# First stage of a Hyena block: another order of loads and blocks, x1 evicted by two engines, its bias added later

## The chip, the cores and the metric

The kernel runs on one core of a Trainium2 chip. The metric is the device time of one execution in microseconds. The engines of the core are TensorE (PE), VectorE (DVE), ScalarE (ACT), GpSimd (POOL) and SyncE (SP); each works through its own instructions in program order and waits on semaphores for the others.

## The reference, cut to what matters

```python
xn = _layernorm(x)                          # x: 4096 tokens x 256 channels
# attention branch: a second layernorm (gamma, beta), then
proj = (layernorm(xn) @ W_in + b_in)        # 256 -> 3 x 256: v, x1, x2
y = v
for kern, xi in ((k0, x1), (k1, x2)):       # 128 taps, causal, one filter per channel
    y = fft_conv(y, kern) * xi
out_attn = xn + (y @ W_out + b_out)
# feed-forward branch: weights are int32 / 127
h = silu(xn @ wg.T) * (xn @ wu.T)           # 256 -> 768
out = x + out_attn + h @ wd.T               # 768 -> 256
```

## The kernel before

Tokens are cut into 32 blocks of 128. The **first stage** goes over the blocks one by one and does four kinds of work.

1. **Blocks.** DVE takes mean and variance of x (`layernorm_stats`, in batches of 4, 8, 8, 8 and 4 blocks, `CUTS`). POOL makes the scales of a batch (`layernorm_scales`, lines 979 to 991; `r_ready` is given at line 987, `r2_ready` at line 991). ACT normalises a block (line 563), PE transposes it (line 290), ACT rounds it to float16 (line 567), DVE takes the remainder (`split_x`, line 703), and ACT writes a copy with reversed token order (`reverse_x`, line 574). PE then projects the block: x1 in `project_x1` (six products of 256 columns), and the first 32 channels of v and x2 in `project` (six products of 64 columns). A block is transposed four steps ahead of its projection (`p = b - 4`).
2. **x1.** DVE evicts x1 block by block (line 713, 256 values per partition): it multiplies by the block's scale, adds the bias row and writes to `x1y2`, where neighbouring channels are 32 values apart. `bias` is itself made by POOL (line 1039).
3. **v and x2.** After every eight blocks DVE scales one bank (line 721), POOL adds a bias (`add_bias`, line 999), ACT rounds (line 579), POOL takes the remainder (`split_v`, line 1005).
4. **Weights and constants.** Column norms of the input weights (PE), their scales (DVE, `column_scales`) and the split in two float16 parts; the filter taps, which POOL scales and splits (`taps`) and SP writes to memory and reads back as bands; the maxima of the FFN weights (DVE, line 816), a chain of tiny DVE operations (`ffn_constants`, lines 759 to 775), and nine pairs of FFN weight tiles. POOL scales a pair (line 1012), PE transposes it (line 323), ACT rounds it (line 583), DVE takes the remainder (line 726). One buffer and one bank hold a pair, so the pairs go one after another.

Whether the FFN weights need a third product is decided on the chip: PE loads a flag that `ffn_constants` makes and takes one of two copies of the code that follows. This branch stands after step 17 of the first stage (`FORK`), so both copies hold the rest of that stage.

The **main loop** goes over 16 groups of 16 channels (G). Each group has two convolutions (bands times v, then bands times y1), three FFN steps of 512 tokens x 128 hidden units, and the projections of later channels. POOL multiplies by x1 (`gate_1`, line 1062, two halves) and by x2 (`gate_2`, line 1068), adds biases for the later channels, and works on the residual (`residual`, lines 1031 and 1032, two blocks a group). The **last stage** projects y to the output and stores it.

All order is written out by hand. SP issues the loads: x in five parts, the taps, the FFN weights, then the two output tensors; ACT issues W_in, gamma, beta and b_in. PE order in step b is: transpose block b, project block b - 4, transpose a pair.

## Time and profile before

| | us |
|---|---|
| median of 3 runs (lowest, highest) | 374.84 (373.56, 377.35) |
| the profiled execution | 376.25 |
| its span, first to last instruction | 374.4 |

| engine | busy us (share of the span) | instructions |
|---|---|---|
| PE | 314.0 (84%) | 4940 |
| DVE | 253.6 (68%) | 522 |
| ACT | 183.2 (49%) | 383 |
| POOL | 196.6 (53%) | 268 |

The shares are means over the three stages. The first stage projects its first block at 28.75 us and its last one until 92.8 us; the first convolution starts at 98.44 us. The last group of the main loop ends near 345 us. So the first stage with its way into the main loop takes about a quarter of the span.

### The profile page before, as it was taken

The numbers are of one execution on the slowest core, as the hardware profiler recorded it, in microseconds if no ns is written. First come the engines' busy times: TensorE is split into PE (matmuls) and PEld (weight loads), VectorE is DVE, ScalarE is ACT, GpSimd is POOL, SyncE is SP. The second block draws the span as 40 slices with busy tenths as digits, with TensorE's granted clock in tenths as the row PEclk, the third lists the DMA queues.
The fourth block names the chain that finished last, engine by engine and source line by source line (L and its number), as shares of the span: only waits on it lengthen the run. The fifth ranks groups of instructions, "written<-read, shape, count | busy, mean of one in ns | idle before, by whom it ended". The sixth has DMA issues, their size and how long they took to land.

```text
span 374.4 us, 11762 instructions
## 1 busy us (share of the span) xinstructions
PE 314.0 (84%) x4940; PEld 244.9 (65%) x4940; DVE 253.6 (68%) x522; ACT 183.2 (49%) x383; POOL 196.6 (53%) x268
## 2 busy tenths in 40 slices
PE   0637593988699889999999999999997997857995
PEld 0426462877477667677777777777765775645994
DVE  1894994788356766666667657667658666576986
ACT  1465363896253434433534444434443344427993
POOL 3697085466566746747657667567564573210000
PEclk9977867899899999999999999999999899996999
DMA  8996100033268758687786786886886768500345
GB/s 251 340 306 218 65 1 4 2 92 137 56 242 374 249 218 320 256 321 279 268 355 237 283 355 227 306 333 222 315 315 247 268 202 339 199 0 3 115 168 170
DMA packets 22072, 81.00 MB, mean 216 GB/s; under 512 B 2050, under 2 KB 13186, under 8 KB 13826
## 3 DMA queue, kind: packets, MB, share of 16 engines
q1 hardware_dynamic: 21026, 79.04, 57.7%
q10 hardware_dynamic: 992, 1.18, 1.0%
q8 instruction: 41, 0.67, 0.7%
q14 instruction: 13, 0.11, 0.1%
HBM read 75.50 MB, written 4.72 MB: 214 GB/s over the span
## 4 chain that ended last, share of the span: by engine, by line
DVE 28%; ACT 18%; POOL 17%; PE 17%; issue 15%; DMA 3%; POOLq 0%; DVEq 0%; SPq 0%; ACTq 0%
PE bank_c L270 6%; DVE sgh L830 6%; ACT hhl L613 5%; DVE vx L721 4%; POOL vx L999 3%; PE bank_g L270 3%; PE bank_u L270 3%; ACT vx L663 3%; POOL x1y L1068 3%; DMA res<-in_L_attn_x 3%; DVE ybuf L851 3%; POOL ybuf L1062 3%; DVE hhl L835 2%; DVE res L842 2%; POOL vhl L1005 2%
## 5 line engine op out<-in xcount | busy, mean ns | idle before, releaser
L270 PE MATMUL bank_d<-wd,hhl 128*128 128x256 f16 x384 | 87.3, 271 | 4.5 <-DVE hhl L835 4.1
L270 PEld LDWEIGHTS bank_p<-wq,xT 128*128 128x128 f16 x1536 | 72.4, 99 | 18.2 <-issue 2.2
L270 PE MATMUL bank_p<-wq,xT 128*128 128x64 f16 x1536 | 82.2, 195 | 1.8 <-issue 1.8
L270 PEld LDWEIGHTS bank_c<-vhl,bands 128*128 128x128 f16 x1024 | 52.7, 98 | 28.5 <-issue 13.4
L270 PE MATMUL bank_c<-vhl,bands 128*128 128x64 f16 (+3 forms) x1024 | 61.4, 187 | 10.2 <-POOL vhl L1005 7.9
L270 PE MATMUL bank_u<-xT,wgu 128*128 128x512 f16 x192 | 66.7, 381 | 0.0
L270 PE MATMUL bank_g<-xT,wgu 128*128 128x512 f16 x192 | 66.7, 381 | 0.0
L270 PEld LDWEIGHTS bank_c<-ybuf,bands 128*128 128x128 f16 x1024 | 51.7, 96 | 19.2 <-issue 3.2
L270 PE MATMUL bank_c<-ybuf,bands 128*128 128x64 f16 (+3 forms) x1024 | 60.1, 184 | 2.7 <-DVE ybuf L855 2.7
L835 DVE TENSOR_TENSOR hhl<-sgh,hhl 128x512 f16<-128x512 f32 x48 | 39.0, 812 | 34.1 <-ACT hhl L613 34.1
L613 ACT CAST hhl<-sgh 128x512 f16<-128x512 f32 x48 | 29.6, 617 | 54.9 <-DVE sgh L830 54.6
L999 POOL TENSOR_TENSOR vx<-vx,bias 128x512 f32<-128x512 f32 x32 | 34.4, 1074 | 41.7 <-DVE vx L721 40.9
L607 ACT ACTIVATE sgh<-bank_g,cst 128x512 f32<-128x512 f32 x48 | 32.7, 681 | 25.7 <-PE bank_g L270 25.6
L270 PEld LDWEIGHTS bank_d<-wd,hhl 128*128 128x128 f16 x384 | 37.0, 97 | 5.9 <-ACT hhl L613 4.4
L270 PE MATMUL bank_c<-wq,xr 128*128 128x256 f16 x192 | 31.3, 308 | 8.3 <-DVE x1y L713 4.5
L1068 POOL TENSOR_TENSOR x1y<-ybuf,vx 128x256 f32<-128x256 f32 x32 | 27.3, 867 | 19.6 <-DVE ybuf L851 19.6
L830 DVE SCALAR_TENSOR_TENSOR sgh<-bank_u,cst,sgh 128x512 f32<-128x512 f32 x48 | 35.6, 742 | 0.0
L851 DVE TENSOR_TENSOR ybuf<-bank_c,xr 128x256 f32<-128x256 f32 x64 | 26.6, 416 | 13.0 <-ACT xr L621 12.5
L1062 POOL TENSOR_TENSOR ybuf<-ybuf,x1y 128x256 f32<-128x256 f32 x32 | 23.3, 728 | 21.2 <-DVE ybuf L851 21.2
L1005 POOL TENSOR_TENSOR vhl<-vx,vhl 128x256 f16<-128x256 f32 x32 | 24.3, 758 | 15.1 <-ACT vhl L579 15.1
L621 ACT COPY xr<-bank_c 128x256 f32<-128x256 f32 x64 | 23.6, 369 | 16.9 <-PE bank_c L270 16.9
L270 PEld LDWEIGHTS bank_c<-wq,xr 128*128 128x128 f16 x192 | 20.5, 111 | 13.6 <-issue 5.3
(167 smaller groups left out, 541.6 us busy)
## 6 DMA issues: line engine op xcount, KB each, us to landing
bands<-taps_seq SPq DMA_DIRECT2D x64, 1024.0 KB, 7.6
out<-res SPq DMA_DIRECT2D x8, 512.0 KB, 2.9
res<-in_L_attn_x SPq DMA_DIRECT2D x3, 1024.0 KB, 10.4
res<-in_L_attn_x SPq DMA_DIRECT2D x2, 512.0 KB, 8.3
bands<-in_L_attn_W_in ACTq DMA_DIRECT2D x1, 768.0 KB, 5.7
bands<-in_L_ffn_w_gate SPq DMA_DIRECT2D x1, 768.0 KB, 10.0
bands<-in_L_ffn_w_up SPq DMA_DIRECT2D x1, 768.0 KB, 10.2
vx<-in_L_ffn_w_down SPq DMA_DIRECT2D x1, 768.0 KB, 10.5
```

What stands on the lines that cost most here:

```text
L270: return nc.tensor.matmul(o, w, m, start=start, stop=stop, skip_group_check=True)
L607: nc.scalar.activation(sgh[:, n % 2, :], bank_g[:, :], ACT.Silu, scale=c(C_GS)).then_inc(sg_ready, 1)
L613: nc.scalar.copy(hhl[:, n % 3, 0, :], sgh[:, n % 2, :]).then_inc(hh_ready, 1)
L621: nc.scalar.copy(conv_lo[:, h, :, :], o[:, 1, :, :]).then_inc(lo_copied, 1)
L721: nc.vector.tensor_tensor(vx[:, r % 2, :, :, blocks].rearrange("p i c b -> p (i c) b"), bank_p[n % 2][:, :].rearrange("p (b c) -> p c b", ...
L830: nc.vector.scalar_tensor_tensor(out=sgh[:, n % 2, :], in0=bank_u[:, :], scalar=c(C_HS), in1=sgh[:, n % 2, :], op0=ALU.mult, op1=ALU.mult) ...
L835: nc.vector.tensor_tensor(hhl[:, n % 3, 1, :], sgh[:, n % 2, :], hhl[:, n % 3, 0, :], ALU.subtract).then_inc(hl_ready, 1)
L851: nc.vector.tensor_tensor(y1f[:, h * CH:(h + 1) * CH, :], o[:, 0, :, :], conv_lo[:, h, :, :], ALU.add).then_inc(c_added, 1)
L999: nc.gpsimd.tensor_tensor(tile, tile, off, ALU.add).then_inc(vx_ready, 1)
L1005: nc.gpsimd.tensor_tensor(vhl[:, r % 2, 1, :, blocks], vx[:, r % 2, 0, :, blocks], vhl[:, r % 2, 0, :, blocks], ALU.subtract).then_inc(vl_ ...
L1062: nc.gpsimd.tensor_tensor(y1f[:, chans, :], y1f[:, chans, :], x1y2[:, G * CG + h * CH:G * CG + (h + 1) * CH, :], ALU.mult).then_inc(y1_rea ...
L1068: nc.gpsimd.tensor_tensor(x1y2[:, G * CG + h * CH:G * CG + (h + 1) * CH, :], y1f[:, h * CH:(h + 1) * CH, :], vx[:, r % 2, 1, g * CG + h * ...
```

## The change

It edits the first stage and one place of the main loop.

- **Loads.** SP issues W_in right behind the first part of x; the parts of x become 4, 4, 8, 8 and 8 blocks, with the taps, w_gate, w_up and w_down between them. ACT issues gamma, beta and b_in only.
- **Order of blocks.** A block is projected eight steps after its transposition (`LAG`) in place of four. The beta product stands before the first block on PE. DVE's statistics are cut into pieces, mostly one block a step. Column scales, taps, the three maxima and the FFN constants stand at other steps, the pairs start at step 20 (`PAIR0`).
- **Second half of the input weights.** POOL multiplies rows 128 to 255 by gamma and by the column scale (two operations) and takes their low part; DVE did both before.
- **Normalising.** Blocks 20 to 31 are normalised by POOL, blocks 0 to 19 by ACT.
- **x1.** Pairs 0 to 5 of blocks are evicted by ACT (a copy with a scale, two of 256 values a pair), pairs 6 to 15 by DVE (one operation of 512 values a pair). No bias is added there.
- **Bias of x1.** POOL adds it in `add_x1_bias`, 512 values for each of the 16 groups: for group 0 behind the first stage, for group G + 1 behind `gate_2` of group G. `gate_1` waits for it.
- **Residual.** The residual of blocks 0 to 3 stands behind the last `split_v` of the first stage.
- **Branch.** PE's branch stands at the stage's end, behind the wait for all pairs.

```diff
-    CUTS = (0, 4, 12, 20, 28, NB)
+    CUTS = (0, 4, 8, 16, 24, NB)
+    LAG = 8
+    NA = 20
+    JA = 6
+    PAIR0 = 20
...
+            load_x(0)
+            sp.dma_start(win[:, :, :], W_in.rearrange("(k p) n -> p k n", p=P)).then_inc(win_loaded, 16)
+            load_x(1)
+            load_x(2)
...
-                p = b - 4
-                if p >= 0:
+                p = b - LAG
+                if 0 <= p < NB:
                     project_x1(p)
...
             def body(general):
-                for b in range(FORK, NB + 4):
-                    first_stage(b)
-                pe.wait_ge(unit_h, PAIRS)
-                pe.wait_ge(unit_l, PAIRS)
                 for G in range(NG):
...
-            FORK = 17
-            for b in range(FORK):
+            beta_weights()
+            for b in range(NB + LAG):
                 first_stage(b)
+            pe.wait_ge(unit_h, PAIRS)
+            pe.wait_ge(unit_l, PAIRS)
...
+            def evict_x1(j):
+                act.wait_ge(x1_mm, 2 * j + 2)
...
+                    last = nc.scalar.activation(x1y2[:, :, b:b + 1].rearrange("p c o -> p (c o)"), o, ACT.Copy, scale=col(r2r, b))
+                last.then_inc(x1a_ready, 1)
...
-                nc.vector.scalar_tensor_tensor(out=x1y2[:, :, b:b + 1].rearrange("p c o -> p (c o)"), in0=o, scalar=col(r2r, b),
-                                               in1=bias[:, D:2 * D], op0=ALU.mult, op1=ALU.add).then_inc(x1_ready, 1)
...
+                nc.vector.tensor_tensor(x1y2[:, :, pair], bank_c[j % 2][:, :].rearrange("p (b c) -> p c b", b=2), scales,
+                                        ALU.mult).then_inc(x1v_ready, 1)
...
-            for b in range(1, NB + 7):
-                if b in (3, 10, 13):
-                    layernorm_stats({3: 2, 10: 3, 13: 4}[b])
+            for b in range(1, NB + LAG + 5):
+                if b == 1:
+                    layernorm_stats(4, 8)
+                elif b in (2, 3, 4):
+                    layernorm_stats(3 * b + 2, min(3 * b + 5, 16))
+                elif b + 11 < NB:
+                    layernorm_stats(b + 11, b + 12)
...
+            def normalise(b):
...
+                pool.wait_ge(x_tp, b - 3)
+                nc.gpsimd.tensor_scalar(xn[:, b % 4, :], res[:, b, :], col(r1, b), col(nmr, b), ALU.mult, ALU.add).then_inc(xnp_ready, 1)
...
+            def add_x1_bias(G):
...
+                nc.gpsimd.tensor_tensor(tile, tile, off, ALU.add).then_inc(x1_biased, 1)
...
+                if b == 21:
+                    layernorm_scales(4)
+                if NA <= b + 2 < NB:
+                    normalise(b + 2)
...
+            add_x1_bias(0)
...
+                pool.wait_ge(x1_biased, G + 1)
...
+                if G < NG - 1:
+                    add_x1_bias(G + 1)
```

Two places in the instruction order carry most of the prediction. POOL from the first pair on (line 1012 before, line 1057 now; the names `lns` are layernorm scales, `vx` is the pair's buffer or a bank of v and x2, `ybuf` the normalised block). Before:

```order
L1012 TENSOR_SCALAR vx<-bands,cst 128x512 x2
L1005 TENSOR_TENSOR vhl<-vx,vhl 128x32x8
L1012 TENSOR_SCALAR vx<-bands,cst 128x512
L999 TENSOR_TENSOR vx<-vx,bias 128x64x8
L1012 TENSOR_SCALAR vx<-bands,cst 128x512 x3
```

Now:

```order
L1057 TENSOR_SCALAR vx<-bands,cst 128x512
L1022 TENSOR_SCALAR lns<-mv 128x8
L1023 TENSOR_TENSOR lns<-lns,minus_half 128x8
L1024 TENSOR_TENSOR lns<-mv,lns 128x8
L1025 TENSOR_SCALAR lns<-lns 128x8
L1026 TENSOR_TENSOR lns<-mv,lns 128x8
L1027 TENSOR_TENSOR lns<-lns 128x8
L1028 TENSOR_SCALAR lns<-lns 128x8
L1029 TENSOR_TENSOR lns<-lns,minus_half 128x8
L1030 TENSOR_SCALAR lns<-lns 128x8
L1036 TENSOR_SCALAR ybuf<-res,lns 128x256 x2
L1057 TENSOR_SCALAR vx<-bands,cst 128x512
```

Behind the first pair POOL now has a whole batch of scales and then two normalised blocks, where it went from pair to pair before.

PE around the branch (`COMPARE_AND_BRANCH`; `bank_c` takes x1 or a convolution, `bank_p` v and x2, `bank_g` and `bank_u` the FFN). Before:

```order
L323 MATMUL bank_d<-ident,vx 128x128 x4
L503 TENSOR_LOAD flag
L503 ISA x2
L504 COMPARE_AND_BRANCH
L290 MATMUL bank_d<-ident,ybuf 128x128 x2
L270 MATMUL bank_c<-wq,xr 128x256 x6
L270 MATMUL bank_p<-wq,xT 128x64 x6
```

Now:

```order
L282 MATMUL bank_c<-wq,xr 128x256 x6
L282 MATMUL bank_p<-wq,xT 128x64 x6
L523 TENSOR_LOAD flag
L523 ISA x2
L524 COMPARE_AND_BRANCH
L282 MATMUL bank_g<-xT,wgu 128x512 x6
L282 MATMUL bank_u<-xT,wgu 128x512 x6
```

The branch moved from the middle of the blocks to between the last projection and the first FFN step.

## Rows read from the trace of the kernel before

**Rows 1.** busy time by engine in three stretches: length, each engine's busy us (instructions), PEclk, DMA share, GB/s.

```profile
28.75:59.50 30.75, 21.34 (x186) 16.86 (x187) 25.16 (x81) 16.62 (x37) 17.38 (x30) 0.75 0.24 86
63.50:92.80 29.30, 26.71 (x294) 23.77 (x295) 22.55 (x46) 24.65 (x55) 16.93 (x15) 0.93 0.21 74
98.40:344.60 246.20, 228.47 (x4180) 173.83 (x4181) 160.14 (x268) 105.23 (x215) 136.70 (x176) 0.97 0.69 258
```

**Rows 2.** timeline of DVE: start, us, line, operation, out<-in, count, [idle before].

```profile
9.45 0.16 DVE L779 SCALAR_TENSOR_TENSOR gnorm<-gb 128x4 f32<-128x4 f32 x1 [0.81 <-DMA gb<-in_L_attn_beta]
...
15.88 1.02 DVE L735 SCALAR_TENSOR_TENSOR bands<-bank_c,bands 128x384 f32<-128x384 f32 x2
...
53.08 0.17 DVE L759 COPY cst<-bank_d 128x3 f32<-128x3 f32 x1
...
56.88 0.15 DVE L775 TENSOR_SCALAR flag<-cst 128x1 int32<-128x1 f32 x1
```

**Rows 3.** timeline of PE, the same columns.

```profile
14.84 3.58 PE L270 MATMUL bank_p<-bands,vx 128*128 128x384 f32 x8
...
28.75 1.44 PE L270 MATMUL bank_c<-wq,xr 128*128 128x256 f16 x6 [3.83 <-issue]
...
30.78 1.49 PE L270 MATMUL bank_c<-wq,xr 128*128 128x256 f16 x6
...
63.52 0.66 PE L290 MATMUL bank_d<-ident,ybuf 128*128 128x128 f32 x2 [3.49 <-issue]
...
84.28 0.82 PE L270 MATMUL bank_c<-wq,xr 128*128 128x256 f16 x6
...
85.36 0.82 PE L270 MATMUL bank_c<-wq,xr 128*128 128x256 f16 x6
...
92.81 1.03 PE L270 MATMUL bank_g<-xT,wgu 128*128 128x512 f16 x4
...
98.44 2.71 PE L270 MATMUL bank_c<-vhl,bands 128*128 128x64 f16 x64 [3.74 <-POOL vhl L1005]
```

**Rows 4.** timeline of ACT, one block's normalise, round and reverse.

```profile
82.60 0.61 ACT L563 ACTIVATE ybuf<-res,lns 128x256 f32<-128x256 f32 x1
83.10 0.37 ACT L567 CAST xT<-bank_u 128x256 f16<-128x256 f32 x1
...
83.87 0.61 ACT L563 ACTIVATE ybuf<-res,lns 128x256 f32<-128x256 f32 x1
```

**Rows 5.** groups of POOL instructions before 98.4 us: busy us, mean ns, idle before.

```profile
L1012 POOL TENSOR_SCALAR vx<-bands,cst 128x512 f32<-128x512 int32 x6 | 9.4, 1570 | 11.1 <-PE bank_d L323 11.1
...
L999 POOL TENSOR_TENSOR vx<-vx,bias 128x512 f32<-128x512 f32 x4 | 4.3, 1078 | 1.8 <-DVE vx L721 1.8
...
L1031 POOL TENSOR_SCALAR res<-res,lns 128x256 f32<-128x256 f32 x4 | 2.2, 558 | 0.0
...
L1039 POOL TENSOR_TENSOR bias<-vhl 128x768 f32<-128x768 f32 x1 | 1.8, 1814 | 0.0
```

**Rows 6.** durations of line 655 on ACT: ns min/median/max.

```profile
L655 ACT ACTIVATE vx<-x1y,lns x32: 722/796/909, 338.3 to 366.4; 128x256 f32<-128x256 f32 x32
```

**Rows 7.** timeline of POOL, two batches of layernorm scales.

```profile
15.10 0.86 POOL L983 TENSOR_SCALAR lns<-mv 128x8 f32<-128x8 f32 x1 [2.29 <-DVE mv L695]
...
46.78 0.24 POOL L983 TENSOR_SCALAR lns<-mv 128x8 f32<-128x8 f32 x1 [11.13 <-DVE mv L695]
...
49.36 0.24 POOL L987 TENSOR_SCALAR lns<-lns 128x8 f32<-128x8 f32 x1
...
50.49 1.67 POOL L991 TENSOR_TENSOR lns<-lns,minus_half 128x8 f32<-128x8 f32 x1
```

**Rows 8.** timeline of POOL in group 1 of the main loop.

```profile
115.36 0.73 POOL L1062 TENSOR_TENSOR ybuf<-ybuf,x1y 128x256 f32<-128x256 f32 x1
117.05 0.72 POOL L1062 TENSOR_TENSOR ybuf<-ybuf,x1y 128x256 f32<-128x256 f32 x1 [0.96 <-DVE ybuf L851]
```

**Rows 9.** durations of line 835 on DVE: ns min/median/max.

```profile
L835 DVE TENSOR_TENSOR hhl<-sgh,hhl x48: 691/716/1245, 102.1 to 335.3; 128x512 f16<-128x512 f32 x48
```

More of the change, by code:

```diff
@@ L252, in _ @@
                         if G == 0 and v == 0:
-                            sp.wait_ge(wql_ready, 2)
+                            for k in range(KD):
+                                sp.wait_ge(wql_ready[k], 1)
                         elif G == 0:
@@ L562, in normalise @@
                     act.wait_ge(x_tp, b - 3)
[L563 removed]
+                nc.scalar.activation(xn[:, b % 4, :], res[:, b, :], ACT.Identity, bias=col(nmr, b), scale=col(r1, b)).then_inc(xna_ready, 1)
             def round_x(b):
@@ L586, in _ @@
             normalise(1)
-            for b in range(NB + 6):
-                if b + 2 < NB:
+            for b in range(NB + LAG + 5):
+                if b + 2 < NA:
                     normalise(b + 2)
@@ L1059, in gate_1 @@
+            add_x1_bias(0)
+            pool.wait_ge(bout_loaded, 16)
+            for b in range(TPC):
+                residual(b)
             def gate_1(G, h):
```

266 lines of the change are left out of this document (154 added, 112 removed).

## The prediction

> **What bounds the kernel now.** I read the stretches by engine first, then the timelines of PE, ACT, DVE and POOL in the first stage, then POOL's and DVE's rows of the main loop. In the main loop PE is busy 228.5 of 246.2 us [rows 1], so little is to be won or lost there unless a new wait reaches PE. In the first stage PE is busy 21.3 of 30.75 us in the first part and 26.7 of 29.3 us in the second, at a granted clock of 0.75 and 0.93 [rows 1]. The first part is held by DVE, 25.2 of 30.75 us busy, the second by ACT, 24.65 of 29.3 us [rows 1]. ACT's step there is normalise 0.50, then round and reverse 0.77, together 1.27 us a block [rows 4]. PE needs 1.08 us a block at the full clock and 2.03 at the lower level (starts of x1's products at 84.28 and 85.36, at 28.75 and 30.78 [rows 3]). PE also stands still for 3.49 us at the branch, before 63.52 [rows 3]. The end of the stage is the first convolution at 98.44 us, 3.74 us after PE ran dry [rows 3].
>
> **The change, as one path.** I follow the new order along what each step waits for.
>
> 1. *Until the scales of blocks 8 to 15.* DVE starts gamma's norm at 9.45 us, on the arrival of beta [rows 2]. ACT issues these loads one place earlier, which I count as 0.5 us; they may land up to 2.5 us earlier as the large W_in is no longer ahead of them. The column scales start at 15.88 us now [rows 2]. In the new order they stand behind the remainder of block 0, and that stands behind the beta product, 3.58 us [rows 3], which was behind the first transpositions. With the norm products from 11.5 to 12.8 us this gives 12.8 + 3.3 + 1.2 = 17.3 for their start and 19.5 for the scales. Then POOL's second multiplication of 768 values, 1.8 us [rows 5], its small batch (2.2 us to `r_ready`), ACT's block 4 and the two casts, 2.4 us: 25.9. DVE's remaining statistics and the low half, 3.1 us, give 29.0, and POOL's scales of eight blocks take 46.78 to 49.6, 2.8 us [rows 7]: 31.8 at the late end, 29.3 at the early end. I take 30.5, in the middle. This part gives nothing: the first projection follows 1.3 us later, at 31.8, where it is at 28.75 now [rows 3].
> 2. *Steps 6 to 17.* ACT paces: 12 x 1.27 = 15.2 us [rows 4] and four evictions of a pair. The trace shows no ACT copy from a bank to places 32 values apart. Below it is bounded by the 0.26 us that rounding adds to a step, a bank read of the same size (from the 0.77 of rows 4, less a reverse of 0.51), above by 0.80 us for ACT's strided read [rows 6]. I take 0.55, the middle, so 1.1 a pair and 4.4 in all: 50.1. The ends move this by 2 us either way. DVE's pieces fit beside it: its statistics are unchanged in number, its maxima stand in three steps, and from pair 6 on one operation replaces two.
> 3. *The constants.* DVE's chain runs from 53.08 to 57.03 [rows 2], 3.95 us, and comes at step 18, behind 0.5 us of step work: 54.6. Here PE is held for about 2 us, no more, as it is two blocks ahead.
> 4. *Steps 20 to 31.* Now POOL paces. It must do one pair (1.57), a batch of scales (46.78 to 52.16, 5.4 us [rows 7]), nine normalised blocks of 0.56, four more pairs, one bias of 1.08 and one `split_v` of 0.67: 1.57 + 5.4 + 5.0 + 6.3 + 1.1 + 0.7 = 20.0 us [rows 5, 7]. Block 31 is normalised at 74.6, 1.9 us a step up to there, more than ACT's 0.8 and PE's 1.3.
> 5. *Pairs 5 to 8.* POOL and PE take turns on one buffer. Pair 5 ends at 76.2; three more turns of 1.57 for POOL, 0.5 for PE and 0.2 for the signals are 6.8, and the bias between them 1.1: 84.1. PE's transposition, 0.5, and its last two blocks, 2 x 0.83 (1.08 less the transposition's 0.25), end at 86.2. Before it was 92.8.
> 6. *Into the main loop.* The v path needs 0.7 + 1.08 + 0.4 + 0.67 and signals, 3.2 us. It is hidden by PE's own: the branch, 3.49 us [rows 3], then gate and up products, of which four took 1.03 us at the full clock at 92.81 [rows 3], 1.7 to 1.9 for all eight, and 3.4 at the lower level, at which PE came back from this stall. The convolution starts at 86.2 + 6.9 = 93.1, which is 5.3 us earlier. The lower level is then mostly used up: the first 64 products took 2.7 us at 98.44 [rows 3], partly at the lower level, and I estimate 2.0 here, 0.7 less. So 6.0 us are won. The residual of four blocks that held `split_v` now stands behind it: POOL is free at 89.4 + 1.1 + 4 x 1.3 = 95.7, where the first sum is ready at 95.1; the second `gate_1` comes later anyway, so this costs nothing.
> 7. *Main loop.* POOL gets 15 additions of 1.08 us [rows 5]. Today the first `gate_1` of a group follows the residual without idle time and the second has 0.96 us of idle before it [rows 8]. An addition of 1.08 uses up that idle and leaves 0.12 us. Only in the odd groups does the path to PE's next wait go through it: 7 x 0.12 = 0.9 us. The ends are 0 and 15 x 1.08 = 16.2.
>
> Sum: 6.0 - 0.9 = **5.1 us less**. Against the profiled execution, 376.25 us, that is 371.1. The runs shown have their median 1.4 us lower, so I forecast **369.7 us**.
>
> **Two rules beside the rows.** On step 7, DVE's low half of h, line 835, takes 0.69 us at the least and 1.25 us at the most [rows 9], in the same group of instructions, and long ones lie beside POOL's gates. The Trainium skill, page "SBUF — State Buffer", section "SBUF: two separate sides", says that a DVE operation with two SBUF inputs and a GpSimd operation hold one pair of ports for the whole instruction, and that the other is blocked, not slowed. By that rule each added POOL operation could also hold up a DVE one, up to its whole length; it is the second rival below. The trace agrees in kind: 1.25 us is not explained by the operation's size. On step 6 the row shows 3.49 us without work behind the branch. The Trainium skill, page "Runtime: NRT & Kernel Launch", section "Instruction fetch mechanics", says that a taken branch to code outside the window that is held forces a fetch before PE goes on. By it the stall would follow the branch to its new place whatever the code there; the row bears out that there is one.
>
> **The rivals.** (A) The forecast as above: 0.50.
> (B) *The front goes faster*: evictions on ACT at 0.26 us (2 us up to step 17) and gamma and beta early (1.2 us). Everything behind moves, since POOL's work waits for the constants: 369.7 - 3.2 = 366.5. For it speaks that ACT's bank reads are its shortest operations. 0.13.
> (C) *POOL is slower than its own rows.* A small scale operation took 0.86 us at 15.10 beside DVE and 0.24 at 46.78 [rows 7], the same form. Two batches, two multiplications and a subtraction now stand in front of the first projection. Stretched by 2 us there and 2 us in steps 20 to 31, the time is 373.7, no change that can be told. 0.17.
> (D) *The additions reach the path*, with the blocking: 15 x 1.08 = 16.2 in place of 0.9 makes 385.0. The kernel is slower than before from (5.1 + 0.9) / 15 = 0.4 us a group on. Against it speak the idle times of POOL [rows 8]. 0.10.
> (E) *TensorE stays at its lower level.* PE goes idle for up to 4 us at POOL's batch in step 21, and after 3.49 us of idle it came back at the lower level [rows 3]. If it held that over steps 23 to 39, its step would be 2.03 + 0.23 with a transposition and 1.6 + 0.23 without: 62.1 + 9 x 2.3 + 8 x 1.83 = 97.4 as the stage's end in place of 86.2, and 380.9 in all. It decides against the change from half of these steps on. Against it: at the lower level PE would be busy all the time, and in such a stretch from 63.5 us on it returned to the full clock (0.93 over the stretch [rows 1]). 0.10.
>
> **How the numbers follow.** Of a kernel like this a measurement can tell about 1% from no change, 3.7 us, so faster is below 371.1 and slower above 378.6. A's own range is 366 to 373; 0.45 of its 0.50 lie below 371.1. With B that is 0.58. Within 1% are C, the rest of A and 0.05 of the mild forms of D and E: 0.27. The rest, 0.15, is slower. The range takes in B and, for the unsure length of steps 20 to 39, 3 us below it, 363.5, and on the other side C and the mild forms of D and E, up to 378.5; beyond the two ends lie some 0.15 to 0.2.
>
> **What would show it.** In the trace after: the first projection near 32 us, later than now; ACT without gaps up to about 50 us; POOL nearly without idle time from 55 to 76 us, with PE waiting for its normalised blocks; PE's last projection near 86 us, then 3.5 us of nothing, then the FFN step at the lower level and the convolution near 93 us; in the main loop the second `gate_1` right behind the first one and the loop's length as now, 246 us, within 2 us. A first projection beyond 35 us, an eviction on ACT of 0.8 us, or a loop longer by over 4 us would each take most of the gain; the forecast is wrong as well if PE's stall at the branch is not there.

## The result, and the profile after

| | before | after |
|---|---|---|
| median of 4 runs (lowest, highest) | 374.20 (372.04, 377.35) | 379.97 (378.27, 381.08) |
| ratio | | 1.011, interval 1.006 to 1.016 |
| the profiled execution; its span | 376.25; 374.4 | 378.27; 376.5 |
| first projection | 28.75 | 34.62 |
| first convolution | 98.44 | 97.80 |
| two groups of the main loop | 29.04 | 29.81 |

The kernel became slower by about 1%, where I forecast 369.7 us. By the ratio the change costs 4 us (2 to 6); the two profiled executions are 2.0 us apart, since that of before was above its median and that of after was the lowest of its four. "Two groups" is the distance of two token maxima of y on DVE (line 860 before, 898 after), which repeat in the main loop: 13.86 + 15.18 us before, 14.19 + 15.62 us after. Single groups are longer in either trace (16.70 us once before), so I compare the repeating pair. From the first maximum to the last it is 220.2 us before and 222.9 after, 2.7 us more; the long group before hides 1.5 us of the difference, and seven repeating pairs would make 5.4.

The stretches by engine, as in [rows 1] (length, busy us, PEclk, DMA share, GB/s), from the first projection to the end of steps 6 to 19, then to the last projection, then the main loop:

```profile
34.62:60.00 25.38, 18.85 (x191) 15.79 (x192) 22.42 (x73) 22.59 (x52) 17.03 (x26) 0.83 0.30 105
60.00:90.40 30.40, 25.17 (x287) 22.46 (x284) 18.06 (x36) 18.03 (x39) 25.66 (x31) 0.94 0.20 70
97.80:347.00 249.20, 229.33 (x4183) 173.33 (x4182) 157.27 (x269) 105.60 (x216) 159.47 (x195) 0.98 0.68 255
```

ACT holds the first stretch (22.59 of 25.38 us) beside DVE, and POOL the second (25.66 of 30.40 us, 16.93 of 29.3 us before), as forecast. In the last one PE is busy 229.3 us as before, but the stretch is 249.2 us long and not 246.2, and POOL's busy time went from 136.7 to 159.5 us.

PE's timeline (start, us, line, operation, count, [idle before]):

```profile
12.96 4.17 PE L282 MATMUL bank_p<-bands,vx 128*128 128x384 f32 x8
...
34.62 1.44 PE L282 MATMUL bank_c<-wq,xr 128*128 128x256 f16 x6 [0.18 <-ACT xr L593]
...
66.33 0.44 PE L305 MATMUL bank_d<-ident,ybuf 128*128 128x128 f32 x2 [3.97 <-POOL ybuf L1036]
...
90.05 0.34 PE L282 MATMUL bank_p<-wq,xT 128*128 128x64 f16 x6
94.46 1.89 PE L282 MATMUL bank_g<-xT,wgu 128*128 128x512 f16 x4 [4.08 <-issue]
...
97.80 1.89 PE L282 MATMUL bank_c<-vhl,bands 128*128 128x64 f16 x64
```

The beta product takes 4.17 us (3.58 before, 14.84 in [rows 3]). The first projection comes at 34.62. The wait for POOL's normalised block, 3.97 us before 66.33, is there, and so is the idle time at the branch, 4.08 us, at its new place behind the last projection. The FFN products behind it run at the lower level (1.89 for four, 1.03 at 92.81 in [rows 3]), and the convolution starts without a wait.

DVE's timeline at the front:

```profile
17.79 0.42 DVE L735 TENSOR_TENSOR xT<-bank_g,xT 128x256 f16<-128x256 f32 x1 [4.42 <-ACT xT L586]
18.13 1.01 DVE L767 SCALAR_TENSOR_TENSOR bands<-bank_c,bands 128x384 f32<-128x384 f32 x2
...
20.36 1.02 DVE L773 SCALAR_TENSOR_TENSOR bands<-bands,gb,vhl 128x768 f32<-128x768 f32 x1
...
58.37 0.15 DVE L805 TENSOR_SCALAR flag<-cst 128x1 int32<-128x1 f32 x1
```

The remainder of block 0 comes at 17.79, after 4.42 us of idle time, and the column scales at 18.13 (15.88 in [rows 2]). The constants end at 58.52.

POOL's timeline in the first stage:

```profile
20.48 2.57 POOL L1101 TENSOR_TENSOR bands<-bands,vhl 128x768 f32<-128x768 f32 x1 [6.58 <-DVE vhl L771]
...
33.03 0.21 POOL L1026 TENSOR_TENSOR lns<-mv,lns 128x8 f32<-128x8 f32 x1
...
58.62 1.56 POOL L1057 TENSOR_SCALAR vx<-bands,cst 128x512 f32<-128x512 int32 x1 [0.38 <-DVE flag L805]
...
78.08 0.55 POOL L1036 TENSOR_SCALAR ybuf<-res,lns 128x256 f32<-128x256 f32 x1
```

The new second multiplication took 2.57 us. It began at 20.48, while DVE's operation at 20.36, with two inputs in SBUF, still had until about 21.35 to run; behind that it took 1.7 us, near the 1.81 us of the same size in [rows 5]. The scales of blocks 8 to 15 are ready at 33.1 us. From the first pair at 58.62 to the end of the last normalised block at 78.63 it is 20.0 us.

ACT's eviction of a pair:

```profile
42.94 1.19 ACT L601 ACTIVATE x1y<-bank_c,lns 128x256 f32<-128x256 f32 x2
```

Groups of POOL's instructions in the main loop (count, busy us, mean ns, idle before):

```profile
L1142 POOL TENSOR_TENSOR ybuf<-ybuf,x1y 128x256 f32<-128x256 f32 x32 | 25.3, 808 | 3.6 <-DVE ybuf L889 3.6
L1094 POOL TENSOR_TENSOR res<-res,bout 128x256 f32<-128x256 f32 x30 | 24.5, 815 | 2.5
...
L1085 POOL TENSOR_TENSOR x1y<-x1y,bias 128x512 f32<-128x512 f32 x15 | 15.7, 1045 | 0.0
```

Line 1142 is `gate_1`. Before (line 1062) it had 21.2 us of idle time ahead of it in 32 instructions and a mean of 728 ns; now 3.6 us and 808 ns. The addition to the residual (line 1094) has a mean of 815 ns in place of 730. So POOL got 15.7 us of additions, and by the means 32 x 0.080 + 30 x 0.085 = 5.1 us more for 62 instructions that are as long as before when nothing is beside them.

One pair of groups on POOL: an addition, a residual and the gates in the first group, a residual and the gates in the second:

```profile
201.47 1.04 POOL L1085 TENSOR_TENSOR x1y<-x1y,bias 128x512 f32<-128x512 f32 x1
...
204.48 1.07 POOL L1094 TENSOR_TENSOR res<-res,bout 128x256 f32<-128x256 f32 x1
205.51 1.41 POOL L1142 TENSOR_TENSOR ybuf<-ybuf,x1y 128x256 f32<-128x256 f32 x2
...
218.68 0.72 POOL L1094 TENSOR_TENSOR res<-res,bout 128x256 f32<-128x256 f32 x1
219.36 1.86 POOL L1142 TENSOR_TENSOR ybuf<-ybuf,x1y 128x256 f32<-128x256 f32 x2
```

and DVE's low half of h (line 873) beside them:

```profile
204.28 0.69 DVE L873 TENSOR_TENSOR hhl<-sgh,hhl 128x512 f16<-128x512 f32 x1 [0.68 <-ACT hhl L643]
...
218.87 1.07 DVE L873 TENSOR_TENSOR hhl<-sgh,hhl 128x512 f16<-128x512 f32 x1 [0.68 <-ACT hhl L643]
```

In the first group DVE's operation starts first, at 204.28, and POOL's at 204.48 takes 1.07 us and not 0.73. In the second, DVE's at 218.87 starts beside POOL's at 218.68 and takes 1.07 us and not 0.69, and then POOL's two gates take 1.86 us and not 1.41. From the start of `gate_2` to the end of the second `gate_1` it is 7.27 and 7.39 us; before the change it was 6.95 us in both groups, with the 0.96 us of idle time in it [rows 8].

Where that idle time came from decides what an addition costs. POOL's first gate in the same two groups of the kernel before:

```profile
204.58 0.73 POOL L1062 TENSOR_TENSOR ybuf<-ybuf,x1y 128x256 f32<-128x256 f32 x1
...
218.45 0.72 POOL L1062 TENSOR_TENSOR ybuf<-ybuf,x1y 128x256 f32<-128x256 f32 x1
```

and DVE's low half of h (line 835 there) beside it:

```profile
204.66 1.19 DVE L835 TENSOR_TENSOR hhl<-sgh,hhl 128x512 f16<-128x512 f32 x1 [0.69 <-ACT hhl L613]
...
218.95 0.77 DVE L835 TENSOR_TENSOR hhl<-sgh,hhl 128x512 f16<-128x512 f32 x1 [0.68 <-ACT hhl L613]
```

DVE's operation starts 0.08 us behind the gate in one group and 0.50 us in the other, and ends 0.54 and 0.55 us behind the gate's end. DVE's eviction of 0.41 us follows it, and the second gate waits for that: together the 0.96 us. So the idle time was no reserve. It hangs on the first gate and moves with it, as long as the gate starts ahead of DVE's low half. In the change DVE's low half starts first in both groups, the idle time is gone, and POOL's operations are the ones that take longer.

### The profile page after: what moved, and what is told of

It reads as the page before. It is cut to its first block, busy times and chain, and to the rows that moved or that the text cites. A ratio compares the mean times of both kernels' runs of the same rounds, so it can differ in the third digit from the quotient of the medians.

```text
span 376.5 us, 11807 instructions
## 1 busy us (share of the span) xinstructions
PE 314.4 (84%) x4940; PEld 244.0 (65%) x4940; DVE 240.8 (64%) x498; ACT 182.6 (48%) x383; POOL 228.0 (61%) x299
## 4 chain that ended last, share of the span: by engine, by line
POOL 33%; DVE 21%; PE 16%; ACT 14%; issue 12%; DMA 2%; ACTq 0%; POOLq 0%; DVEq 0%
POOL x1y L1148 5%; POOL ybuf L1142 5%; PE bank_c L282 5%; DVE vx L753 4%; POOL vx L1044 4%; POOL res L1093 3%; DVE sgh L868 3%; POOL vx L1057 3%; POOL x1y L1085 3%; ACT hhl L643 3%; PE bank_p L282 3%; ACT vx L693 3%; POOL res L1094 3%; PE bank_g L282 2%; PE bank_d L282 2%
## 5 line engine op out<-in xcount | busy, mean ns | idle before, releaser
L282 PEld LDWEIGHTS bank_p<-wq,xT 128*128 128x128 f16 x1536 | 71.6, 99 | 17.3 <-issue 1.6
L282 PEld LDWEIGHTS bank_c<-vhl,bands 128*128 128x128 f16 x1024 | 51.3, 96 | 26.3 <-issue 10.5
L282 PE MATMUL bank_c<-vhl,bands 128*128 128x64 f16 (+3 forms) x1024 | 59.9, 184 | 8.6 <-POOL vhl L1050 6.0
L873 DVE TENSOR_TENSOR hhl<-sgh,hhl 128x512 f16<-128x512 f32 x48 | 36.4, 759 | 37.4 <-ACT hhl L643 37.4
L1148 POOL TENSOR_TENSOR x1y<-ybuf,vx 128x256 f32<-128x256 f32 x32 | 28.2, 896 | 17.4 <-DVE ybuf L889 17.4
L893 DVE SCALAR_TENSOR_TENSOR ybuf<-ybuf 128x512 f16<-128x512 f32 x16 | 11.1, 692 | 31.3 <-ACT ybuf L657 31.3
L282 PE MATMUL bank_c<-wq,xr 128*128 128x256 f16 x192 | 28.8, 291 | 2.0 <-ACT x1y L601 1.8
L651 ACT COPY xr<-bank_c 128x256 f32<-128x256 f32 x64 | 23.6, 369 | 11.8 <-PE bank_c L282 11.6
L1094 POOL TENSOR_TENSOR res<-res,bout 128x256 f32<-128x256 f32 x32 | 25.9, 810 | 2.7
```

The lines of the kernel that those rows point to most:

```text
L282: return nc.tensor.matmul(o, w, m, start=start, stop=stop, skip_group_check=True)
L651: nc.scalar.copy(conv_lo[:, h, :, :], o[:, 1, :, :]).then_inc(lo_copied, 1)
L873: nc.vector.tensor_tensor(hhl[:, n % 3, 1, :], sgh[:, n % 2, :], hhl[:, n % 3, 0, :], ALU.subtract).then_inc(hl_ready, 1)
L1094: nc.gpsimd.tensor_tensor(res[:, b, :], res[:, b, :], bout[:, :], ALU.add).then_inc(bout_added, 1)
L1148: nc.gpsimd.tensor_tensor(x1y2[:, G * CG + h * CH:G * CG + (h + 1) * CH, :], y1f[:, h * CH:(h + 1) * CH, :], vx[:, r % 2, 1, g * CG + h * ...
```

## The experiments

A ratio is to the kernel before in runs on the same chip. "Convolution" is the start of the first convolution, "two groups" as above, both in the profiled execution.

| kernel | median us | ratio (interval) | convolution | two groups |
|---|---|---|---|---|
| the change | 379.97 | 1.011 (1.006 to 1.016) | 97.80 | 29.81 |
| 1 addition behind gate_1 | 376.77 | 1.003 (1.001 to 1.005) | 100.36 | 29.39 |
| 2 before, with additions | 379.98 | 1.015 (1.011 to 1.018) | 98.41 | 29.83 |
| 3 front as before | 373.78 | 0.996 (0.993 to 0.999) | 93.78 | 29.82 |
| 4 before, branch at the end | 369.68 | 0.986 (0.984 to 0.988) | 95.13 | 29.03 |
| 5 ACT normalises all | 377.58 | 1.004 (1.001 to 1.008) | 97.42 | 29.82 |
| 6 no additions | 377.26 | 1.007 (1.002 to 1.011) | 100.84 | 29.05 |
| 8 = 6 and 3 | 372.26 | 0.993 (0.988 to 0.997) | 96.93 | 29.02 |
| 9 = 8 and 5 | 370.60 | 0.988 (0.983 to 0.993) | 95.71 | 29.06 |
| 10 small addition | 370.65 | 0.991 (0.987 to 0.995) | 92.58 | 29.45 |
| 11 before, two operations | 395.78 | 1.058 (1.050 to 1.067) | 98.98 | 32.13 |
| 12 beta product alone | 374.56 | 1.001 (0.997 to 1.005) | 94.27 | 29.83 |
| 13 additions in idle time | 370.13 | 0.988 (0.984 to 0.993) | 94.57 | 29.02 |

### The main loop: what an addition costs

**1. The addition behind the gates.** The same work at another place of POOL's order, behind `gate_1(G, 1)`.

```diff
+                if G < NG - 1:
+                    add_x1_bias(G + 1)
...
                 gate_2(G, 1)
-                if G < NG - 1:
-                    add_x1_bias(G + 1)
```

> The changed kernel, with the addition of x1's bias for group G + 1 moved from behind gate_2 to behind gate_1 of group G, where POOL waits about 2.07 us for DVE in every group. Same 15 additions, same lengths. Theory 1 (place): the addition of 1.04 us stands in the one stretch of POOL that closes a ring with the other engines (gate_2, residual, gate_1), uses up the 0.96 us of idle that was there, and lets POOL set the pace of every group; moved into the wait, two groups take 29.0 us again in place of 29.8, and the kernel is 5 to 6 us faster than the changed one, about 374 to 375. Theory 2 (ports): the additions cost by holding up DVE or being held up, wherever they stand; then two groups stay near 29.8 us and the time near 380.

More than half of the added time is gone from the loop: 29.39 us in place of 29.81 (29.04 before). So theory 1 is right on the place but not on the size, and the time, 376.77 us, is above its 374 to 375. POOL's gates and then the addition:

```profile
207.91 0.73 POOL L1142 TENSOR_TENSOR ybuf<-ybuf,x1y 128x256 f32<-128x256 f32 x1 [0.96 <-DVE ybuf L889]
208.60 1.05 POOL L1085 TENSOR_TENSOR x1y<-x1y,bias 128x512 f32<-128x512 f32 x1
```

The 0.96 us of idle time is back. The rest of 0.35 us lies on DVE, whose operation on y1 starts beside the addition:

```profile
209.34 0.86 DVE L893 SCALAR_TENSOR_TENSOR ybuf<-ybuf 128x512 f16<-128x512 f32 x1 [1.51 <-ACT ybuf L657]
```

It takes 0.86 us and not 0.69, in both groups, and POOL's next work waits for it. The first stage was 2.6 us later here than in the changed kernel though nothing differs in it: the beta product took 4.86 us and not 4.17, and TensorE's granted clock was 0.73 from 70 to 80 us, where it was 0.93 at the same place (69 to 79 us) in the change. The profiled execution, 378.0 us, is the slowest of the ten, so the median holds less of this.

**2. The additions alone**, put into the kernel before, at the place that they have in the changed one (behind `gate_2(G, 1)`).

```diff
-                nc.vector.scalar_tensor_tensor(out=x1y2[:, :, b:b + 1].rearrange("p c o -> p (c o)"), in0=o, scalar=col(r2r, b),
-                                               in1=bias[:, D:2 * D], op0=ALU.mult, op1=ALU.add).then_inc(x1_ready, 1)
+                nc.vector.tensor_scalar(x1y2[:, :, b:b + 1].rearrange("p c o -> p (c o)"), o, col(r2r, b), None, ALU.mult).then_inc(x1_ready, 1)
...
+            add_x1_bias(0)
...
+                if G < NG - 1:
+                    add_x1_bias(G + 1)
```

> The kernel before, with one part of the change alone: DVE evicts x1 without the bias (one operation a block as before, 32 of them), and POOL adds it group by group, for group 0 behind the first stage and for group G + 1 behind gate_2 of group G. Nothing else moves. Theory 1: two groups of the main loop go from 29.04 to 29.8 us, seven pairs of groups make 5.4 us, so about 379.6 against 374.2. The prediction's own figure for this part was 0.9 us, so 375. If the time is like before's, the loss of the changed kernel's loop comes from something else (the other residual order, the code's position).

1.015, with two groups at 29.83 us: the additions alone give the whole of the loop's loss, and the time is the 379.6 us of theory 1 within 0.4 us. The first convolution is where it was before (98.41 us). The ratio is above the change's 1.011, but the two intervals overlap, so whether the rest of the change won anything in all can't be told from them.

**6. No additions** in the changed kernel; DVE evicts all of x1 with its bias.

```diff
-    JA = 6
+    JA = 0
...
-                nc.vector.tensor_tensor(x1y2[:, :, pair], bank_c[j % 2][:, :].rearrange("p (b c) -> p c b", b=2), scales,
-                                        ALU.mult).then_inc(x1v_ready, 1)
+                for b in (2 * j, 2 * j + 1):
...
+                    last = nc.vector.scalar_tensor_tensor(out=x1y2[:, :, b:b + 1].rearrange("p c o -> p (c o)"), in0=o, scalar=col(r2r, b),
+                                                          in1=bias[:, D:2 * D], op0=ALU.mult, op1=ALU.add)
...
-                if G < NG - 1:
-                    add_x1_bias(G + 1)
```

> The changed kernel with x1 evicted by DVE block by block with its bias, as before, and no addition on POOL anywhere (ACT evicts nothing). Theory 1 (POOL's additions lengthen the main loop by stretching its ring): the interval of two groups returns from 29.8 to 29.0 us, 5.4 us less. The first stage: ACT loses six pairs of 1.18 us, DVE gets twelve blocks of 0.5 us more; if ACT paced steps 6 to 17 alone, the constants end up to 7 us earlier (51.5 in place of 58.5), if DVE does next, 2 us earlier. Together 369 to 373 us. Rival 3 (the longer loop comes from something else of the change, such as code placed elsewhere or the branch): the interval stays at 29.8 and the time is 375 or more.

The loop is back at 29.05 us, as theory 1 has it. The expected time was missed: the convolution came at 100.84, 3 us later than in the changed kernel, and not earlier. PE's longest waits in steps 8 to 28:

```profile
49.56 0.47 PE L373 MATMUL bank_d<-ident,pmw 128*128 128x128 f32 x1 [4.63 <-DVE pmw L856]
...
62.56 0.66 PE L305 MATMUL bank_g<-ident,ybuf 128*128 128x128 f32 x2 [2.92 <-DVE xT L735]
```

Both are for DVE, and both are longer than in the change (3.0 and 1.7 us). With about 1.14 us a pair on DVE beside its three maxima and the constants, DVE is busy 28.5 of the 30 us from 30 to 60 us, and the constants end at 61.5 us (58.5 in the change). By these two traces the evictions of the change, on ACT and without bias, were worth 3 us.

**11. Two operations a group** in the kernel before, which keeps its bias at the eviction: it is added and subtracted again.

```diff
+                link(nc.gpsimd.tensor_tensor(tile, tile, off, ALU.add))
+                nc.gpsimd.tensor_tensor(tile, tile, off, ALU.subtract).then_inc(x1_biased, 1)
```

> The kernel before, which adds the bias at eviction, with two operations of 512 values on POOL for every group behind gate_2: the bias is added and subtracted again, one after the other. One addition made two groups longer by 0.77 us and the time by 5 us. Theory 1 (0.96 us of idle time a group is used up by the first one, and the ring of POOL is then the bound): the second, about 1.1 us with its semaphore, costs its whole length in every group, two groups take about 32 us, the time is about 395 us. Rival 2 (each addition costs by the DVE operation that it delays, 0.36 us): 30.6 us for two groups and 385 us.

395.78 us, as theory 1 has it. Each group is longer than before by 1.54 us. The second operation costs 2.3 us in two groups, its length with its signal (1.12 us) each time, where the first cost 0.77 to 0.79 us. POOL's order in this kernel, from the second operation on:

```profile
211.19 1.05 POOL L1035 TENSOR_TENSOR x1y<-x1y,bias 128x512 f32<-128x512 f32 x1
212.23 0.55 POOL L1040 TENSOR_SCALAR res<-res,lns 128x256 f32<-128x256 f32 x1
...
213.58 0.99 POOL L1040 TENSOR_SCALAR res<-res,lns 128x256 f32<-128x256 f32 x1
...
215.33 1.41 POOL L1073 TENSOR_TENSOR ybuf<-ybuf,x1y 128x256 f32<-128x256 f32 x2
```

There is no idle time left, and the residual at 213.58 took 0.99 us beside DVE (0.55 otherwise). Rival 2 is out.

**10. A small addition**: ACT's 12 blocks only, 192 values a group. The front and the normalising are as in 3 and 5.

```diff
-                tile = x1y2[:, G * CG:(G + 1) * CG, :]
+                tile = x1y2[:, G * CG:(G + 1) * CG, 0:2 * JA]
```

(DVE's eviction of blocks 12 to 31 is that of 6.)

> The changed kernel with the column scales and the beta product where they were before, ACT normalising all 32 blocks, and the bias at eviction wherever DVE evicts (blocks 12 to 31), so that POOL's addition covers 12 blocks: 192 values a group in place of 512. Theory 1 (what counts is the addition's length against POOL's idle time of 0.96 us in a group): about 0.45 us long, it fits; two groups take 29.0 to 29.1 us in place of 29.8. With the front's 6 us and 2.4 us for the normalising: 366 to 368 us. Rival 2 (any further operation in POOL's ring costs, by its start and its semaphores): 29.4 us and about 370 us.

The numbers, 29.45 and 370.65 us, are rival 2's, but its mechanism, a price in every group, is not what the trace shows; theory 1 missed both. The addition takes 0.51 us, less than the idle time, and costs nothing in one group (13.79 us, 13.86 before) and 0.48 in the next (15.66 us, 15.18 before). POOL there, the gates of the longer group and then the addition and the gates of the shorter one:

```profile
211.97 0.73 POOL L1145 TENSOR_TENSOR ybuf<-ybuf,x1y 128x256 f32<-128x256 f32 x1
213.66 0.73 POOL L1145 TENSOR_TENSOR ybuf<-ybuf,x1y 128x256 f32<-128x256 f32 x1 [0.96 <-DVE ybuf L892]
...
224.46 0.51 POOL L1088 TENSOR_TENSOR x1y<-x1y,bias 128x192 f32<-128x192 f32 x1
...
227.64 1.87 POOL L1145 TENSOR_TENSOR ybuf<-ybuf,x1y 128x256 f32<-128x256 f32 x2
```

DVE, in the first of the two groups:

```profile
212.00 1.25 DVE L876 TENSOR_TENSOR hhl<-sgh,hhl 128x512 f16<-128x512 f32 x1 [0.69 <-ACT hhl L644]
213.17 0.41 DVE L892 TENSOR_TENSOR ybuf<-bank_c,xr 128x256 f32<-128x256 f32 x1
```

At 211.97 POOL's gate starts 0.03 us ahead of DVE's low half. DVE's operation then takes 1.25 us and not 0.69, the eviction for the second gate starts at 213.17, and the 0.96 us of idle time is there again, behind the gate, as in the kernel before: the addition has moved all of it by its own length. In the shorter group the gates follow each other without idle time, as in the change: 1.87 us in place of 0.73 + 0.96 + 0.73 = 2.42, which is 0.55 us less and pays for the addition's 0.51. So the price of an operation in this ring is not its length less the idle time. It depends on which of the two engines starts first behind it.

**13. The additions in idle time** of the first stage: 8 blocks in one operation at step 18, 4 blocks at step 38, none in the loop; otherwise as 10.

```diff
+                if b == 18:
+                    add_x1_bias(0, 8)
...
+                if b == 38:
+                    add_x1_bias(8, 2 * JA)
```

> The small-addition kernel, with the bias of the 12 blocks that ACT evicts added by POOL inside the first stage: blocks 0 to 7 in one operation of 2048 values at step 18 (about 4.2 us, where POOL was idle for 4.8 us before its first split_v), blocks 8 to 11 in one of 1024 values at step 38 (about 2.1 us, where it was idle for 4.0 us). Nothing is added in the main loop. Theory 1 (an operation on POOL costs what it adds to a ring and nothing in an idle stretch): two groups take 29.05 us as before the change, the first convolution stays near 92.6 us, the time is 367 to 368.5 us. Rival 2 (the long addition holds up DVE's chain of constants, and so the first pair): the constants end 1 to 2 us later, the time is 369 to 370 us.

The loop is at 29.02 us, and the convolution at 94.57 us, 2 us later than in 10. Rival 2 was right in kind: 370.13 us, though the constants end 2.5 us later than in 10 (56.2 and 53.7) and not 1 to 2. The two timelines show why. POOL:

```profile
48.48 3.73 POOL L1086 TENSOR_TENSOR x1y<-x1y,bias 128x2048 f32<-128x2048 f32 x1 [0.68 <-ACT x1y L602]
52.31 0.67 POOL L1053 TENSOR_TENSOR vhl<-vx,vhl 128x256 f16<-128x256 f32 x1
56.28 1.57 POOL L1060 TENSOR_SCALAR vx<-bands,cst 128x512 f32<-128x512 int32 x1 [3.30 <-DVE flag L809]
```

DVE in the same stretch:

```profile
48.66 0.41 DVE L724 BATCH_NORM_STATS2 stats<-res 128x6 f32<-128x256 f32 x1
...
49.52 0.15 DVE L793 COPY cst<-bank_d 128x3 f32<-128x3 f32 x1
49.70 2.53 DVE L715 TENSOR_SCALAR cst<-cst 128x3 f32<-128x3 f32 x1
52.27 0.18 DVE L716 RECIPROCAL cst<-cst 128x3 f32<-128x3 f32 x1
52.48 0.53 DVE L717 TENSOR_SCALAR cst<-cst 128x3 uint32<-128x3 uint32 x1
```

The addition runs from 48.48 to 52.21. Beside it DVE's statistics, remainder and copy from a bank take their usual time. Its operation on **three numbers** at 49.70, from SBUF to SBUF, takes 2.53 us; in kernel 10 the same one took 0.17 us. It ends at 52.23, with POOL's. The next one of the kind, at 52.48, ends at 53.01, with POOL's `split_v` (52.31 to 52.98). This chain makes the constants for which the first pair waits, so 2.5 of POOL's 3.73 us, "in idle time", lie on the path.

The Trainium skill, page "SBUF — State Buffer", section "SBUF: two separate sides", says that DVE and GpSimd share one pair of ports, held for the whole of an instruction by whichever came first, and that a DVE operation takes part if it has two inputs in SBUF or is of a kind that can use both ports, `tensor_scalar` among them. The trace agrees: the one at 49.70 was held to the end of POOL's, and the statistics with one input were not.

### The first stage

**3. The front as before**: the column scales ahead of the statistics and of block 0's remainder, the beta product at step 2.

```diff
+                if b == 2:
+                    beta_weights()
...
-            beta_weights()
             for b in range(NB + LAG):
...
+                    column_scales()
                 elif b in (2, 3, 4):
...
-                if b == 1:
-                    column_scales()
```

> The changed kernel, with the front in the old order: DVE makes the column scales before the statistics of blocks 4 to 7 and before the remainder of block 0, and PE takes the beta product in step 2, not before the first transposition. Theory A: the first stage is late because the column scales wait 4.4 us for the remainder of block 0; they come 4 to 5 us earlier, the first projection goes from 34.6 to about 30.5, the constants from 58.5 to about 55, the first convolution from 97.8 to about 94, and the kernel is 3.5 to 4 us faster than the changed one (376). Theory B: POOL's own chain in front of the first projection (second multiplication, two batches of scales, subtraction) is as long without it; then at most 1 us is gained.

6.2 us less than the change by the medians and 5.6 by the ratios, where I expected 3.5 to 4: the first projection is at 30.03 (34.62), the constants at 53.7, the convolution at 93.78. The traces show 4.0 us at the convolution and 4.8 in the span; medians of two sets of runs of one kernel differ by 1 us (those of before do), which is about what is left.

**12. The beta product alone** at step 2; the column scales keep their new place.

```diff
+                if b == 2:
+                    beta_weights()
...
-            beta_weights()
             for b in range(NB + LAG):
```

> The changed kernel with the beta product at step 2, behind three transpositions, as before; the column scales keep their new place behind the remainder of block 0. Theory A (the beta product of 3.8 to 4.9 us ahead of the first transposition holds the remainder and so the column scales): they start near 14.5 in place of 18.1 us, the first projection comes near 31 us, the time is 375 to 376 us. Theory B (the place of the column scales on DVE behind statistics and remainder is what costs): the first projection stays beyond 33.5 us, the time above 378 us.

Theory A. On DVE:

```profile
13.97 0.42 DVE L736 TENSOR_TENSOR xT<-bank_g,xT 128x256 f16<-128x256 f32 x1 [0.39 <-ACT xT L587]
14.31 1.01 DVE L768 SCALAR_TENSOR_TENSOR bands<-bank_c,bands 128x384 f32<-128x384 f32 x2
```

The remainder of block 0 comes at 13.97 in place of 17.79 and the scales at 14.31 in place of 18.13, 3.8 us earlier, and the first projection at 30.82 (34.62). With this one move the change is level with the kernel before: 1.001 (0.997 to 1.005). Of the 4.6 us that 3 won at the first projection, 3.8 are the beta product and 0.8 the place of the scales on DVE.

**5. ACT normalises all blocks** in the changed kernel.

```diff
-    NA = 20
+    NA = 32
```

> The changed kernel with ACT normalising all 32 blocks; POOL loses 12 operations of 0.56 us. Theory 1 (POOL's own sum paces steps 20 to 31: 20.0 us from 58.6 to 78.6): POOL's sum falls to 15.0 us, ACT then does blocks 24 to 31 from the scales of the last batch on (about 63.5 us) at 1.27 us each, ready at 74; the last pair and the last projection end near 86 in place of 90.4, the time falls by 4 us to about 376. Rival 2 (the turns of PE and POOL on the one pair buffer pace the stage, whoever normalises): the last projection stays within 1 us of 90.4 and the time within 1 us of 380. PE's idle of 3.97 us before 66.3 should go by theory 1.

Rival 2 holds for the stage, though the mechanism is nearer to theory 1's than its number: PE's wait for the normalised block is gone, and in its place stands one of the same length for the pair,

```profile
67.31 1.12 PE L345 MATMUL bank_d<-ident,vx 128*128 128x128 f32 x4 [3.90 <-POOL vx L1057]
```

because POOL's batch of scales, 5.4 us, stands ahead of the second pair in either kernel. The turns of the one pair buffer then fill the time to 90 us. The last projection ended 0.8 us earlier and the convolution came 0.4 us earlier. So the 5.0 us of POOL's normalising were hidden behind turns that come anyway. The time, 377.58 us, lies between the two answers: the ratio fell from 1.011 to 1.004, more than the trace accounts for. That stays open.

**4. The branch at the stage's end** in the kernel before.

```diff
-            FORK = 17
+            FORK = NB + 4
```

> The kernel before, with one part of the change alone: PE's branch stands behind the first stage in place of behind step 17. Theory: in the middle it costs 3.49 us of stall, some 2 us at the lower level of TensorE's clock behind it, and the wait for the FFN constants; at the end it costs the stall and a slower FFN step, together 6.9 to 7.5 us from the last projection to the convolution where it was 5.6. Net about 3.5 us faster than before, 370.5 to 371. Rival: ACT, which paces the second half, and the nine pairs of FFN weights make up for the stall by themselves in the old place, so taking it away gives under 2 us, and the end costs as much: no change or 1 to 2 us slower.

The lowest ratio of this study, 0.986 (9 and 13, at 0.988, can't be told from it). PE's timeline at the stage's end:

```profile
91.77 1.86 PE L270 MATMUL bank_g<-xT,wgu 128*128 128x512 f16 x4 [3.71 <-issue]
...
95.13 1.91 PE L270 MATMUL bank_c<-vhl,bands 128*128 128x64 f16 x64
```

The stall is about as long as before, 3.71 us (3.49), but it now covers the wait of 3.74 us for the v path (98.44 in [rows 3]): the convolution starts at 95.13, 3.3 us earlier, with no wait of its own. By the median the kernel is 5.5 us faster than before, 369.68 us where 370.5 to 371 was expected. The profiled execution, 372.65 us, is the slowest of the five and shows 3.6 us of it; where the rest comes from isn't shown.

The Trainium skill, page "Runtime: NRT & Kernel Launch", section "Instruction fetch mechanics", says that a taken branch to code outside the window that is held forces a fetch first. The trace agrees as far as it goes: the idle time followed the branch here and in the change, to code of another kind.

**8 and 9. Combinations.** 8 has no additions and the front as before; 9 is 8 with ACT normalising all (the last line of the diff).

```diff
-    JA = 6
+    JA = 0
...
+                if b == 2:
+                    beta_weights()
...
-    NA = 20
+    NA = 32
```

> The last kernel, and with it the column scales before the statistics and the remainder of block 0, and the beta product at step 2, as before. If the two faults of the change are independent, the 6.2 us that the second edit gave alone come on top of the last kernel: about 366 us, with the first convolution near 90 us. If POOL's idle time absorbs one of them, 369 us or more.

8 took 372.26 us and not 366. The second edit gave 5.0 us on top of 6, so the two are nearly independent (the convolution came 3.9 us earlier here and 4.0 us earlier in 3), but 6 stood 4 us above the end of its expectation, and 8 carries that.

> The last kernel, with ACT normalising all blocks as well. If POOL paces steps 20 to 31 there too, 3 to 4 us below the last one, about 363 us. If ACT, at 1.27 us a block without pairs to evict, is now the slower one, no difference (within 1 us).

9 took 370.60 us, 1.7 less than 8 (1.2 at the convolution): between the two answers. In both DVE holds the steps up to the constants (28.6 of 30 us busy between 30 and 60 us in 9; 25.3 in 10, where ACT evicts the first pairs).

## Why the prediction was wrong

Two steps of the sum failed: step 1, whose front came 2.6 us too late, and step 7, whose idle time did not take up the addition. The first is a size, the second a mechanism.

- **Step 1, the front, mis-sized by 2.6 us.** "I take 30.5, in the middle": it was 33.1, beyond even the late end of 31.8. The beta product took 4.17 us and not the 3.3 of the sum (3.58 in [rows 3]), so the column scales started at 18.13 and not at 17.3. The second multiplication took 2.57 and not 1.8, as it started beside DVE's operation at 20.36. The batch, the casts and the low half behind them were 0.3 us shorter than counted. I had a sum of rows at the late end and took the middle, for an earlier landing of beta that came to 0.3 us. And 12 shows what I didn't ask: the beta product ahead of the transpositions costs 3.8 us by itself.
- **Steps 2 and 3, right in kind, 1.1 us too short.** An eviction pair on ACT took 1.18 us (1.1 forecast), and ACT was busy nearly all the time. From the first projection to the constants it was 23.9 us, 22.8 forecast; the constants ended at 58.5 and not at 54.6.
- **Step 4, right to the tenth:** 20.0 us from the first pair to the last normalised block. But 5 shows that its parts may not be taken as prices: without the 5.0 us of normalising the stage is 0.4 us shorter.
- **Step 5, right:** from there to the end of the last projection 11.8 us, 11.6 forecast. It ended at 90.4 and not at 86.2, by the front's delay.
- **Step 6, right but for 0.5 us.** The idle time stands at the branch's new place (4.08 us, 3.49 taken), the eight FFN products took 3.3 us at the lower level (3.4), the wait for the v path is gone, and the first 64 products of the convolution took 1.89 us (2.0 taken). 4 shows that this part alone is worth 1.4% of the time. The stage won 0.6 us in place of 5.3.
- **Step 7, the main loop, failed.** "An addition of 1.08 uses up that idle and leaves 0.12 us. Only in the odd groups": every group became longer, by 0.33 and 0.44 us in turn. The step took the 0.96 us for a reserve behind which the addition disappears. But the idle time lies behind the first gate and follows from it (0.54 us of DVE's held operation and 0.41 of the eviction), and the addition stands ahead of that gate. Kernel 10 shows the step's error by itself: an addition of 0.51 us, well below 0.96, costs 0.48 in every second group, with the idle time back in full. The long addition did remove the idle time, because DVE's low half now starts ahead of the gates; in exchange POOL's later operations take 0.34 and 0.45 us longer beside it, and less than 0.1 us is what the addition is longer than the idle time. My second rule named the lock; I counted it as a rival in which DVE is held, with the full length of an addition as its price. In the change it is POOL that loses by it, in every group, and by less.

Rival C came true at the front (POOL slower than its rows, 0.8 us, beside DVE), not in steps 20 to 31. Rival D came true in kind and at a part of its 16.2 us: 2.7 in the two traces, 5.4 by seven repeating pairs and by kernel 2. Its bound, "slower than before from 0.4 us a group on", is near the measured 0.39, but the bound counted on 5.1 us won elsewhere, and they weren't. Rival E did not come in the change: after the wait of 3.97 us PE was back at the full clock between 70 and 72 us (0.94 over the stretch). In the profiled execution of kernel 1 it came in part, as said there. Rival B's eviction at 0.26 us did not come either.

The two traces add up as follows, after less before: 0.6 us less up to the convolution, 0.4 less from there to the first maximum of y, 2.7 more up to the last one, 0.5 more behind it. That is 2.1 us, the difference of the spans. The ratio says 4 us (2 to 6). The long group in the trace of before accounts for 1.5 us of what is between; the rest isn't shown. Against the forecast of 5.1 us less, 4.7 us were lost before the convolution (97.8 and not 93.1), and the loop lost 2.7 to 5.4 us where 0.9 was counted. Alone, the additions cost 1.5% of the time (2), the beta product's new place 1.0% (12 against the change), and the branch's new place gives back 1.4% (4).

## What to carry to other kernels

Before idle time is counted as a reserve, ask what ends it, and whether that itself depends on the operation just ahead of the idle time. If it does, whatever is put in front of both moves both. Where two engines hold each other up, as GpSimd and VectorE do here, look also at what the later operations will then lie beside, group by group, as the trace has it, and price that shift. In kernel 13 this held even for a stretch in which GpSimd had nothing to do: VectorE had a chain of tiny operations on the path there, and one long GpSimd operation held it for 2.4 us. Where the sum of a path has an end that is all rows and another that is a hope, take the rows; and where an added step stands at the head of a path, ask for its cheapest place before pricing the rest.

## What the hardware showed beyond that

- In kernel 13 VectorE's operation on 3 values took 2.36 us longer beside GpSimd's on 2048 values (2.53 and 0.17 us), while its statistics (0.41 us), remainders from a bank (0.39 us) and a copy from a bank (0.15 us) beside the same operation took their usual time.
- The engine that started first kept its time, even by hundredths of a microsecond: with GpSimd 0.03 us ahead (kernel 10), VectorE's 0.69 us became 1.25; with VectorE 0.20 us ahead (the change), GpSimd's 0.73 us became 1.07.
- In the kernel before, VectorE's operation ended 0.54 to 0.55 us behind the end of GpSimd's gate whether it had started 0.08 or 0.50 us behind the gate's start.
- The idle time at the branch was 2.46 to 3.72 us in the middle of the blocks (three kernels) and 3.71 to 4.59 us at the stage's end; behind it TensorE was at the lower level for the eight products in most of the latter (in kernels 9 and 10 the first four took 1.14 and 1.53 us in place of 1.89).
- GpSimd's addition of 192 values took 0.51 us (kernel 10), of 512 values 1.04 (the change), of 1024 values 2.05 and of 2048 values 3.73 us (kernel 13).
